# Edge loop of a graph network on one core: rows scattered plainly and summed in a second pass, instead of added in memory

## The reference

```python
    row, col = (edge_index[0], edge_index[1])          # source, destination of each edge
    h = jnp.concatenate([x[col], edge_attr], axis=1)   # 64 + 64 features
    h = jax.nn.relu(h @ W1.T + b1)                     # 128
    h = jax.nn.relu(h @ W2.T + b2)                     # 128
    summed = jax.ops.segment_sum(h, row, num_segments=n)
    cnt = jax.ops.segment_sum(jnp.ones((h.shape[0],), dtype=h.dtype), row, num_segments=n)
    agg = summed / jnp.maximum(cnt, 1.0)[:, None]
    z = jnp.concatenate([x, agg, u[batch]], axis=1)
    z = jax.nn.relu(z @ Wa.T + ba)
    x = _layernorm(x + z @ Wb.T + bb)
```

## Time and profile before

| What | us |
|---|---|
| Median of three runs | 3785.15 |
| Profiled execution, its own time | 3782.62 |
| Span of its trace | 3780.9 |
| PE busy | 2841.0 (75%) |
| VectorE (DVE) busy | 2309.4 (61%) |
| GpSimd (POOL) busy | 2317.7 (61%) |
| ScalarE (ACT) busy | 1471.8 (39%) |
| Edge loop's scatters, 816, busy on POOL | 1268.6 |

### The profile page before, as it was taken

One profiled execution on the slowest core, in us unless ns is written; L12 is line 12 of the kernel. 1 busy time (PEld: TensorE's weight loads), 2 busy tenths in 40 slices (PEclk: granted clock), 3 DMA queues, 4 the chain that ended last, 5 costly groups with the idle time before them and its releaser, 6 DMA issues. The chain is left out here.

```text
span 3780.9 us, 76143 instructions
## 1 busy us (share of the span) xinstructions
PE 2841.0 (75%) x16134; PEld 2000.5 (53%) x16135; DVE 2309.4 (61%) x8562; ACT 1471.8 (39%) x3352; POOL 2317.7 (61%) x1835
## 2 busy tenths in 40 slices
PE   7267777777777776566699888877878787788763
PEld 4146555555555554442344466666666565666551
DVE  7299999999999997673422354443443443444433
ACT  2055555555555554431000143433433333333331
POOL 0277777777777776510000068888888888888882
PEclk7566666666656665568799889989988988989886
DMA  4544444444444437857034245555555555555544
GB/s 135 102 113 116 128 115 121 122 115 132 120 112 131 115 101 85 101 144 225 3 110 121 71 49 53 54 53 53 54 54 53 54 54 53 54 54 54 54 45 92
DMA packets 659312, 337.65 MB, mean 89 GB/s; under 512 B 434560, under 2 KB 622771, under 8 KB 658228
## 3 DMA queue, kind: packets, MB, share of 16 engines
q0 software_dynamic: 148736, 86.57, 23.9%
q1 hardware_dynamic: 445046, 110.07, 14.2%
q10 hardware_dynamic: 65248, 138.05, 9.8%
HBM read 156.36 MB, written 202.84 MB: 95 GB/s over the span
## 5 line engine op out<-in xcount | busy, mean ns | idle before, releaser
L2183 POOL DMA_INDIRECT sums<-el_rows,el_idx x816 | 1268.6, 1555 | 616.8 <-DVE el_rows L2397 368.6
L822 POOL DMA_INDIRECT at_hs<-table,at_rec_s x976 | 1041.5, 1067 | 444.1 <-PE near_ps L963 216.1
L860 ACT CAST at_count_s<-near_ps 128x400 f16<-128x400 f32 x976 | 482.9, 495 | 732.5 <-PE near_ps L963 644.6
L963 PE MATMUL near_ps<-at_pair_hot,at_src_low_hot 128*128 128x425 f16 x976 | 482.1, 494 | 338.5 <-ACT at_count_s L860 265.7
L2395 DVE CAST el_idx<-el_place 128x4 uint32<-128x4 f32 x204 | 34.8, 171 | 832.5 <-DMA sums<-el_rows,el_idx 812.0
L935 PEld LDWEIGHTS sums_ps<-at_hw,at_hit 128*128 128x128 f32 x1952 | 467.9, 332 | 19.0 <-issue 14.4
L935 PE MATMUL sums_ps<-at_hw,at_hit 128*128 128x66 f32 x1952 | 442.4, 408 | 8.3 <-DVE acc L1009 8.3
L963 PEld LDWEIGHTS near_ps<-at_pair_hot,at_src_low_hot 128*128 128x128 f16 x976 | 134.3, 138 | 485.3 <-ACT at_count_s L860 339.2
L2331 ACT ACTIVATE el_h<-el_h_ps,el_valid 128x128 f32<-128x128 f32 x816 | 232.5, 368 | 248.1 <-PE el_h_ps L2245 248.1
L1001 DVE TENSOR_SCALAR at_pair_hot<-iota_wide,at_rec_s 128x400 f16<-128x400 f16 x976 | 322.4, 333 | 1.4
L1009 DVE SCALAR_TENSOR_TENSOR acc<-acc,at_fade,sums_ps 128x66 f32 x976 | 266.5, 273 | 57.0 <-PE sums_ps L935 52.7
(11 more groups left out here) (374 smaller groups left out, 4980.1 us busy)
## 6 DMA issues: line engine op xcount, KB each, us to landing
slots<-at_count_s ACTq DMA_DIRECT2D x122, 850.0 KB
el_rec<-attr SPq DMA_DIRECT2D x816, 32.0 KB
chunk<-slots SPq DMA_DIRECT2D x256, 100.0 KB
chunk<-slots ACTq DMA_DIRECT2D x208, 100.0 KB
attr<-in_edge_attr SPq DMA_DIRECT2D x16, 1248.0 KB
at_rec_s<-meta SPq DMA_DIRECT2D x976, 3.5 KB
at_hs<-table,at_rec_s POOLq DMA_INDIRECT x976
el_pair<-meta SPq DMA_DIRECT2D x816, 1.0 KB
```

The costliest lines, as they stand in the source:

```text
L822: pool.indirect_dma_start(hs[:, s, u, :], None, k.table, bass.IndirectOffsetOnAxis(rec[:, s, u, 0:1].bitcast(U32), 0)).then_inc(gathered[s ...
L860: a.copy(count[:, (n.o + d) % 2, i, 0:AW], near[:, (n.o + d) % 2, 0:AW]).then_inc(count_ready, 1)
L963: pe.matmul(near[:, s, 0:SW], low_hot[:, s, i, :], pair_hot[:, s, i, :], start=False, stop=True, skip_group_check=(i > 0)).then_inc(near_r ...
L2183: pool.indirect_dma_start(k.sums_flat[a], bass.IndirectOffsetOnAxis(idx[:, j, a:a + 1], 0), rows[:, j, a, :], None, compute_op=ALU.add).th ...
```

## The change

The sum per source moves out of the edge loop into a second pass, `tile_sums`, with a memory table `edge_rows` of 576 B rows between them: 128 numbers of `h2`, the number of the source within its tile, and 15 words of filling.

- In `finish_attention` PE counts the edges of each of the 25 source tiles from the degrees. VectorE rounds each count up to units of 512 rows, which gives each tile a run of rows in the table, and derives for 220 units the first row and the tile.
- In `message_layers` POOL clears the last unit of each of the 25 runs (25 transfers of 288 KB).
- In `edge_loop` an edge's place is its tile's first row plus the number of edges of that tile before it. VectorE compares each edge's tile with 25 numbers (`hot`, 128x200), adds up along the eight visits (`upto`, a scan), and PE adds up over the 128 partitions (`rank_ps`, two small products); `run` carries the counts on. Every edge has a row of its own, so nothing is joined, the source numbers are not spread, `join_rows` is gone, and ScalarE's second relu writes the rows for POOL directly. POOL still issues 816 indirect scatters of 128 rows, without addition, behind two waits for each quad. The feature and second-product banks in PSUM become double.
- `tile_sums` reads the 220 units with transfers issued by SP and ScalarE in turn, five buffers deep. VectorE makes a comparison of the source number with 128 columns (128x512), PE multiplies it with the rows (four float32 products into one bank), and VectorE adds the bank to its tile in `sums`, which stays in SBUF.
- `joins_of`, `hand_over` and `join_rows` are gone (their removed lines are not repeated below). The four tables, their clearing in `attention`, and their loads and additions in `node_update` are gone.

```diff
-SPARE = NP
-NACC = 4
+UNIT = 4 * P
+Q2 = (EP + NT * (UNIT - 1)) // UNIT
+HR = 144
+JUNK = Q2 * UNIT
+LAP = 20
+LOADS = 5
 BIG = float(2.0 ** 100)
 SLOPE = 0.2
...
-            for a in range(NACC):
-                for i in range(8):
-                    sp.dma_start(k.sums_flat[a].rearrange("(p r) h -> p (r h)", p=P)[:, i * ZW:(i + 1) * ZW],
-                                 k.zero[:]).then_inc(sums_zeroed, 16)
...
+            dve.wait_ge(total_ready, 1)
+            step(v.memset(none[:], 0.0))
+            step(v.memset(tile_of[:], 0.0))
+            step(v.tensor_scalar(total[:], total_ps[:, 0:NT], float(UNIT - 1), None, ALU.add))
+            step(v.tensor_copy(units_i[:], total[:]))
+            step(v.tensor_single_scalar(units_i[:], units_i[:], 9, ALU.arith_shift_right))
+            step(v.tensor_copy(units[:], units_i[:]))
+            step(v.tensor_tensor_scan(unit_end[:], units[:], none[:], 0.0, ALU.add, ALU.add))
+            step(v.tensor_tensor(k.row_base[:], unit_end[:], units[:], ALU.subtract))
+            step(v.tensor_scalar(k.row_base[:], k.row_base[:], float(UNIT), -1.0, ALU.mult, ALU.add))
+            step(v.tensor_scalar(total[:], unit_end[:], -1.0, 0.0, ALU.add, ALU.max))
+            step(v.tensor_scalar(total[:], total[:], float(UNIT), None, ALU.mult))
+            step(v.tensor_copy(k.last_row[:], total[0:1, :]))
+            for t in range(NT):
+                step(v.scalar_tensor_tensor(tile_of[:], k.iota_wide[:, 0:Q2], unit_end[:, t:t + 1], tile_of[:], ALU.is_ge,
+                                            ALU.add))
+            step(v.tensor_copy(k.quad_tile[:], tile_of[0:1, :]))
+            step(v.tensor_scalar(tile_of[:], k.iota_wide[:, 0:Q2], float(UNIT), total[:, NT - 1:NT], ALU.mult, ALU.min))
+            step(v.tensor_copy(k.quad_row[:], tile_of[0:1, :]))
...
+            pe.matmul(total_ps[:, 0:NT], k.ones_f[:], k.out_deg[:], start=True, stop=True).then_inc(total_ready, 1)
...
+            clear = k.zero_b[:].bitcast(F32)[:, 0:192].unsqueeze(1).to_broadcast([P, 3, 192])
+            for t in range(NT):
+                pool.dma_start(k.edge_rows[bass.ds(at[t], UNIT), :].rearrange("(p r) f -> p (r f)", p=P)
+                               .rearrange("p (a b) -> p a b", b=192), clear).then_inc(rows_cleared, 16)
+            pool.wait_ge(rows_cleared, 16 * NT)
...
-        sp.dma_start(k.el_pair[:, s, u, :], k.meta[bass.ds(offs[u], P), 2:4]).then_inc(k.el_loaded[s], 16)
+        sp.dma_start(k.el_pair[:, s, u, :], k.meta[bass.ds(offs[u], P), 2:7]).then_inc(k.el_loaded[s], 16)
...
-            def body(it, first):
+            def body(it):
                 for j in range(4):
-                    pool.wait_ge(rows_ready, it * 4 + (j + 1))
+                    s, h = j // 2, j % 2
+                    pool.wait_ge(idx_ready, it * 2 + (s + 1))
                     pool.sem_inc(passed, 1)
-                    for a in range(NACC):
-                        if not (first and j == 0):
-
-                            pool.wait_ge(added[a], it * 64 + 16 * j)
-                            pool.sem_inc(passed, 1)
-                        pool.indirect_dma_start(k.sums_flat[a], bass.IndirectOffsetOnAxis(idx[:, j, a:a + 1], 0),
-                                                rows[:, j, a, :], None, compute_op=ALU.add).then_inc(added[a], 16)
-            body(0, True)
+                    pool.wait_ge(rows_ready, it * 8 + (2 * j + 2))
+                    pool.sem_inc(passed, 1)
+                    for u in range(4):
+                        pool.indirect_dma_start(k.edge_rows, bass.IndirectOffsetOnAxis(idx[:, s, 4 * h + u:4 * h + u + 1], 0),
+                                                rows[:, j, u, :], None).then_inc(scattered[j], 16)
+
+            nc.gpsimd.memset(rows[:], 0.0).then_inc(rows_clear, 1)
+            nc.gpsimd.tensor_copy(before_by[:], k.below[:]).then_inc(constants, 1)
+            nc.gpsimd.tensor_copy(all_by[:], k.ones_f[:]).then_inc(constants, 1)
+            body(0)
             with pool.Fori(1, IT) as it:
-                body(it, False)
-            for a in range(NACC):
-                pool.wait_ge(added[a], 16 * Q)
+                body(it)
+            for j in range(4):
+                pool.wait_ge(scattered[j], 64 * IT)
...
-                pe.wait_ge(ends_ready, m + 1)
-                if not first:
-                    pe.wait_ge(join_ready, m)
-                for u in range(B):
-                    t = pe.transpose(src_t[:, u, :], ends[:, s, u, 0:1].to_broadcast([P, P]), k.ident[:])
-                t.then_inc(src_t_ready, 1)
+
+            def ranks(m, s, first):
+
+                pe.wait_ge(own_ready, m + 1)
+                if first:
+                    pe.wait_ge(constants, 2)
+                else:
+                    pe.wait_ge(first_ready, m * 2)
+                pe.matmul(rank_ps[:, 0, :], before_by[:], own[:, s], start=True, stop=True)
+                pe.matmul(rank_ps[:, 1, :], all_by[:], own[:, s], start=True, stop=True).then_inc(rank_ready, 1)
...
-                    pe.wait_ge(ea_copied, q)
+                    pe.wait_ge(ea_copied, q - 1)
...
-                    pe.wait_ge(h2_done, q)
-                pe.matmul(h2_ps[:], k.ones_b[:], k.b2_parts[:].rearrange("i u h -> i (u h)"), start=True, stop=False)
+                    pe.wait_ge(rows_ready, q * 2 - 2)
...
                         turn_ends(it * 2 + (s + 1), 1 - s, False)
+                        ranks(it * 2 + (s + 1), 1 - s, False)
                     if not (last and j >= 2):
                         turn_features(q + 2, (j + 2) % 4, it * (32 * B) + 32 * B * (1 if s == 0 else 2), False)
-                    if h == 0 and not (first and j == 0):
-                        join_rows(q - 1, (j - 1) % 4, it * 2 + (s + h), first and j < 3)
...
-            def relu2(q, j, n1, first):
+            def relu2(q, j, n1, done):
                 s, h = (j // 2) % 2, j % 2
+                act.wait_ge(low_ready, n1)
+                if done is not None:
+                    act.wait_ge(scattered[j], done)
+                a.copy(rows[:, j, :, H:H + 1], src_low[:, s, 4 * h:4 * h + 4].unsqueeze(2)).then_inc(rows_ready, 1)
                 act.wait_ge(h2_ready, q + 1)
-                act.wait_ge(join_ready, n1)
-                if not first:
-                    act.wait_ge(sum_ready, q - 1)
-                for u in range(4):
-
-                    m = a.activation(h2[:, j % 2, u, :], h2_ps[:, u * P:(u + 1) * P], ACT.Relu,
-                                     scale=valid[:, s, 4 * h + u:4 * h + u + 1])
-                m.then_inc(h2_done, 1)
+                a.activation(rows[:, j, :, 0:H], h2_ps[:, j % 2, :].rearrange("p (u h) -> p u h", h=H), ACT.Relu
+                             ).then_inc(rows_ready, 1)
...
+                ch(v.tensor_scalar(low[:, s], near[:, s], 0.0, None, ALU.is_ge))
...
+                ch.wait()
                 ch.step(v.scalar_tensor_tensor(valid[:, s], near[:, s], float(P), low[:, s], ALU.is_lt, ALU.mult))
+                ch(v.scalar_tensor_tensor(tile_mark[:, s], ends[:, s, :, 4], 1.0, valid[:, s], ALU.add, ALU.mult))
+                if not start:
+                    dve.wait_ge(rows_ready, m * 4 - 4)
+                v.scalar_tensor_tensor(src_low[:, s], ends[:, s, :, 4], -float(P), ends[:, s, :, 0], ALU.mult,
+                                       ALU.add).then_inc(low_ready, 1)
+                ch.wait()
+                ch.step(v.tensor_tensor(hot[:, s], tile_mark[:, s].unsqueeze(1).to_broadcast([P, NT, B]),
+                                        k.iota_tile[:].unsqueeze(2).to_broadcast([P, NT, B]), ALU.is_equal))
+                ch.step(v.tensor_tensor_scan(upto[:, s].rearrange("p t u -> p (t u)"), k.tile_new[:].rearrange("p t u -> p (t u)"),
+                                             hot[:, s].rearrange("p t u -> p (t u)"), 0.0, ALU.mult, ALU.add))
+                if not start:
+                    dve.wait_ge(rank_ready, m - 1)
+                v.tensor_copy(own[:, s], upto[:, s, :, B - 1]).then_inc(own_ready, 1)
+
+            def places_of(m, s, done):
+
+                dve.wait_ge(rank_ready, m + 1)
+                v.tensor_tensor(first[:, s], rank_ps[:, 0, :], run[:], ALU.add).then_inc(first_ready, 1)
+                dve.wait_ge(first_ready, m * 2 + 1)
+                v.tensor_tensor(run[:], run[:], rank_ps[:, 1, :], ALU.add).then_inc(first_ready, 1)
+                ch.step(v.tensor_tensor(upto[:, s], upto[:, s], first[:, s].unsqueeze(2).to_broadcast([P, NT, B]), ALU.add))
+                ch.step(v.tensor_tensor(upto[:, s], upto[:, s], hot[:, s], ALU.mult))
+                ch(v.tensor_reduce(place[:, s], upto[:, s].rearrange("p t u -> p u t"), AX, ALU.add))
+                ch.step(v.scalar_tensor_tensor(aside[:, s], valid[:, s], 0.0, k.junk[:, s * B:s * B + B], ALU.is_equal,
+                                               ALU.mult))
                 if done is not None:
+                    for h in range(2):
```

(126 more changed lines are left out.)

149 lines of the change are left out of this document (82 added, 67 removed).

## The result

The changed kernel took **3903.32 us** (median of 4 runs, 3900.47 to 3907.63), the kernel before on the same chip 3784.04 (median of 4): ratio 1.0321, 95% interval 1.0300 to 1.0341. The ratio leaves out the one run of before at 3970.28 us, which fell into a slower state of the chip. The forecast was 3605 us.

| stretch | before | after | difference | predicted |
|---|---|---|---|---|
| to the first scatter | 2199.7 | 2207.7 | +8.0 | 0 |
| first scatter to the end of the last | 1517.2 | 1377.0 | -140.2 | -446 |
| from there to node_update's start (second pass) | 5.4 | 267.8 | +262.4 | +276 |
| node_update and the end | | | -12.3 | -10 |

What follows compares the result with a forecast made beforehand. POOL's scatter-adds were taken to bound the edge loop. 3782.6 - 1517 + 1071 (new loop) + 276 (second pass) - 10 (node_update) = 3603, or 3605 us against the runs' median; range 3515 to 3840.

Steps and rivals of the forecast that it cites:

- The 2.8: Edge loop, PE: from one pair's last product to the next rank products, 2.8 us with only the mask transposes to do.
- The bracket: Edge loop, PE, each half pair: feature transposes 0.53, first product 1.74, second product 1.31 us; counted twice a pair.
- the 0.3 that the forecast had added: Edge loop: 0.3 us a pair above PE's 10.2, for row and index buffers shared by three close limits, giving 10.5.
- PE idle some 2 us ahead of the rank products: Edge loop: expected sign of the forecast in the changed profile, PE released by VectorE, with pairs at 10 to 11 us.
- Rival B: Edge loop: POOL and the wait for indices, rows and counts alternate, 12.8 us a pair, total 3838 us; chance 0.11.
- the ring: Edge loop: next pair's ranks need VectorE's counts, which wait for ScalarE's rows, which need PE's last product; 2.8 us.
- Rival A: Edge loop: POOL's scatter price does not fall, 1.86 us each, total 4050 us, or 4172 with bytes; chance 0.13.
- rival C: Second pass: waits for its loads one at a time, 2.2 us a unit, total 3823 us; chance 0.06.
- The fit of the Trainium skill: Second pass: one transfer takes 2.0 us plus bytes at 436 GB/s; a unit alone 2.7 us, the whole 3929.
- the row: Edge loop before: 816 scatter-adds at 1.553 us minimum and median beside masks, no sign of VectorE slowing POOL; loop 1071 us.
- the rule: Edge loop: some VectorE operations lock GpSimd out for the whole instruction; 10.9 us a pair, loop 1115 us, 44 more.
- POOL's price: Edge loop: a scatter without addition costs what a gather does, 0.947 us, 1.25 with spacing, 10.0 us a pair.

Runs made afterwards that it cites:

- the run with the filler: Changed kernel with eight unused products on zeros put on PE between mask transposes and rank products, all waits kept: 3627.86 us, ratio 0.9598.
- the run of the later ranks: Changed kernel with PE issuing the next pair's two rank products half a pair later, after the first half's products: 3627.62 us, ratio 0.9601.

## Why the prediction was wrong

**The step that failed** is the sentence "So a pair on PE takes 2.8 + 0.25 + 2 x (0.53 + 1.74 + 1.31) = 10.2 us". The 2.8 was right in kind and a little high: from the start of the mask transposes to the ranks it was 2.48 us (2810.82 to 2813.30). The bracket was wrong. It took its durations from one pair at full clock and put them behind a wait of PE in every pair, as if the clock did not depend on it. At the measured clock the two halves with the ranks took 11.05 us in the mean of 100 pairs, where 7.4 was forecast (0.25 and the bracket's 7.16) and 7.42 measured at full clock in the run with the filler. With a wait of 2.5 instead of 2.8 that is 13.55 us for 10.2; less the 0.3 that the forecast had added, about 3.0 us a pair, the 306 in all. The prediction even listed "PE idle some 2 us ahead of the rank products" as a sign that it was right; the sign appeared, and was the fault.

The trace of before held the warning. The earlier trace rows has a clock of 0.89 for a loop whose sample pair ran at 1.00. The sample pair, and the start of the next one, in the windows view of the kernel before:

```profile
2728.20:2738.50 10.30, 10.30 (x85) 7.79 (x86) 1.96 (x7) 4.66 (x9) 8.61 (x6) 1.00 0.53 53
2738.60:2742.90 4.30, 0.24 (x3) 0.05 (x1) 4.01 (x23) 1.14 (x4) 3.69 (x3) 0.73 0.60 65
2743.00:2747.00 4.00, 3.93 (x23) 3.79 (x24) 0.87 (x3) 1.41 (x2) 3.16 (x3) 0.50 0.46 44
```

The next pair, after a gap of 4.2 us, starts at 0.50. There it was free, since POOL took 14.9 us for a pair anyway; without that cover the slow clock had a price. The Trainium skill, TensorE: Matmul & The Clock Gate, section "HAM oscillation — how this bites in real kernels", describes a loop whose every turn makes PE wait so that each turn starts at the low clock. The four windows of one pair above show that pattern with one difference: PE resumed at 0.99 and fell to 0.50 about 1.1 us later. The page was not weighed in the prediction.

**Rival B** had nearly the right number (12.8 us) for a wrong reason: it put the ring and POOL in series at full clock. The run with the filler keeps that ring and takes 10.84. **Rival A** is answered by the scatter's 0.969 us, **rival C** by the second pass's 1.14 us a unit, where C had 2.2. (The fit of the Trainium skill that the prediction sets beside C is given in the section named there for transfers issued by GpSimd; these loads are issued by SP and ScalarE.)

**SBUF.** The prediction weighed a scatter at the row's price against the rule in the Trainium skill, SBUF — State Buffer, "Who interferes with whom", and took the row: 10.5 us a pair against 10.9. Once the clock was cured, 10.87 and 10.84 were measured, and 10.28 with one input moved out of SBUF: the rule was the better guide, though its price came from attention's mean of 1.067 us a gather and fell so near the loop's 1.052 by luck. The row had not contradicted it. In before, 99 of the 102 masks began while a scatter-add was already running, and those scatter-adds took 1.554 us in the mean; only 2 of 816 began inside a mask, and they took 1.66 and 2.18. In the run of the later ranks 100 of the 102 masks had a scatter that began inside them. The masks themselves took 1.22 us either way, so the runs show only GpSimd being held up. And a price of one form was used to judge another.

**What held.** POOL's price: 0.947 taken, 0.969 measured, for the reason given (no addition). The second pass: 1.2 us a unit forecast, (3850.7 - 3599.5)/220 = 1.14 measured, though with the loads and not PE as its limit. node_update: -10 forecast, -12.3 measured. finish_attention: VectorE's new chain took the place of its wait for transfers, and the stage takes no longer (35.2 us between the same two steps, 35.8 before). SP and VectorE stayed covered.

**Left open.** The +8 ahead of the loop: the first scatter starts anywhere from 2199.5 to 2211.8 in the kernels with the change. The delay is there by the end of attention: VectorE's first step of finish_attention starts at 1681.3 in before, at 1690.4 in the changed kernel and at 1686.9 to 1691.9 in all kernels with the change. No run here tells why. And which gap costs the clock: in the changed kernel slow products followed each of the 100 waits for the counts that lasted over 1 us (1.46 to 1.98), while the run with one input in PSUM has gaps of 1.86 and 2.65 us after which the eight products stay at 1.16. The gap's length alone doesn't decide; a shorter filler was not tried.

## What to carry to other kernels

When the engine that sets the pace gets cheaper, sum the next engine's pair at the clock that it will have, not at the one of a sample: if the new order makes PE wait in every turn, compute the turn at half clock too and keep both ends. A wait for another engine's small result is best placed where PE still has large work to issue; if it can't be moved, idle products in the gap are worth a try. Where a granted clock below 1.00 costs nothing now, name what covers it.

## What the runs showed of the hardware

- An indexed scatter of 128 rows of 512 B took POOL 1.553 us with an addition and 0.969 without; 576 B rows without it took 0.969 as well.
- In the pair shown, 1.87 us of idle PE was followed by some 6.5 us at half clock, beginning about 1 us after PE had resumed; the loop's mean clock was 0.71. Eight unused products of 512 columns in the gap (1.67 us recorded) brought the loop to 1.00 and saved 276 us.
- A comparison of 128x1024 with both inputs in SBUF lengthened a plain scatter that began inside it from 0.97 to as much as 1.99 us; a scatter that was already running when it began took 0.97. With one input in PSUM no scatter took over 1.28.
- Loads of 288 KB on two queues moved 253 GB/s with five buffers and 316 with ten.
